# Recommendation tower on one core: products with one selection a chunk, interaction blocks in quarters of 32 rows

## What is computed

```python
e = stack([tbl_f[ids[:, f]] for f in range(39)], axis=1)    # 512 x 39 x 16
# layer 1: all pairs of features, per number d
z = einsum('bmd,bnd->bdmn', e, e).reshape(B, D, 39 * 39)
x1 = einsum('bdp,po->bod', z, W0)                           # 128 outputs
# layer 2: features times the outputs of layer 1
z = einsum('bmd,bnd->bdmn', e, x1).reshape(B, D, 39 * 128)
x2 = einsum('bdp,po->bod', z, W1)
h = concatenate([sum of x1 and x2 over d, dense_ctx], axis=1)   # 272 wide
h = maximum(h @ W_top1 + b_top1, 0)
h = maximum(h @ W_top2 + b_top2, 0)
y = h @ W_top3
```

## Time and profile before

| what | us |
|---|---|
| median of 3 runs | 230.82 (229.24 to 232.3) |
| the profiled execution | 230.19 |
| its span, first to last instruction | 228.6 |
| PE, DVE, ACT, POOL busy | 204.9, 176.5, 167.6, 109.2 |
| first product (L786) | starts at 37.26 |
| last gather (L387) | starts at 141.82 |
| granted clock of TensorE, mean | 0.985 |

### The profile page before, as it was taken

The page is one execution under the profiler, slowest core; times in us unless marked ns, Lnnn a source line. Parts: engine busy times, 40 slices in busy tenths (PEclk is TensorE's granted clock), DMA queues, the critical chain, the costliest instruction groups (busy, mean ns, idle before and its releaser), DMA issues.

```text
span 228.6 us, 4760 instructions
## 1 busy us (share of the span) xinstructions
PE 204.9 (90%) x1715; PEld 156.0 (68%) x1715; DVE 176.5 (77%) x295; ACT 167.6 (73%) x300; POOL 109.2 (48%) x106
## 2 busy tenths in 40 slices
PE   4577956879989998999999899799999999999995
PEld 4577813435556566777787577577778888889794
DVE  0899956999869899999979998798899787532010
ACT  6999465769867999798879998697867575775003
POOL 4788777777777777877777778000000000000000
PEclk9999779999999999999999999999999999999999
DMA  5950000240392591200240000003100000000000
GB/s 143 217 128 7 9 7 6 65 69 6 77 236 66 70 314 29 44 5 7 65 65 7 7 7 7 1 3 94 22 3 0 0 3 0 1 0 3 0 0 3
DMA packets 22015, 10.26 MB, mean 45 GB/s; under 512 B 11576, under 2 KB 20877, under 8 KB 21992
## 3 DMA queue, kind: packets, MB, share of 16 engines
q1 hardware_dynamic: 18728, 9.11, 16.4%
q0 software_dynamic: 3264, 0.84, 3.9%
HBM read 8.63 MB, written 1.31 MB: 44 GB/s over the span
## 4 chain that ended last, share of the span: by engine, by line
PE 60%; DVE 17%; ACT 9%; issue 7%; DMA 4%; POOL 1%; SPq 1%; DVEq 0%; ACTq 0%
PE s_bank L1013 14%; PE side_bank L967 6%; PE side_bank L969 6%; PE side_bank L968 6%; PE g_bank L995 4%; DVE z L786 3%; DVE z_lo L796 3%; DVE w_sb L725 3%; PE b_bank L947 3%; PE side_bank L962 3%; PE side_bank L995 3%; PE side_bank L934 3%; PE side_bank L975 2%; DMA feat<-tbl,ids_sb 2%; PE side_bank L912 2%
## 5 line engine op out<-in xcount | busy, mean ns | idle before, releaser
L387 POOL DMA_INDIRECT feat<-tbl,ids_sb x102 | 109.0, 1069 | 33.3 <-issue 21.9
L575 ACT ACTIVATE z_hi<-z 128x512 fp32r<-128x512 f32 x100 | 61.9, 632 | 10.6 <-DVE z L786 8.7
L786 DVE TENSOR_TENSOR z<-factors,b_bank 128x512 f32<-128x512 f32 x84 | 57.1, 681 | 7.9 <-PE b_bank L947 3.7
L796 DVE TENSOR_TENSOR z_lo<-z,z_hi 128x512 fp32r<-128x512 f32 x84 | 57.8, 688 | 0.3 <-ACT z_hi L575 0.2
L1013 PE MATMUL s_bank<-g,w_sb 128*128 128x128 f32 x312 | 47.5, 279 | 0.0
L1013 PEld LDWEIGHTS s_bank<-g,w_sb 128*128 128x128 f32 x312 | 44.1, 192 | 4.8 <-issue 2.4
L967 PE MATMUL side_bank<-z_hi,w_hi 128*128 128x512 f32 x84 | 42.3, 504 | 0.0
L969 PE MATMUL side_bank<-z_hi,w_lo 128*128 128x512 f32 x84 | 33.2, 396 | 0.0
L968 PE MATMUL side_bank<-z_lo,w_hi 128*128 128x512 f32 x84 | 32.9, 392 | 0.0
L467 ACT ACTIVATE factors<-side_bank 128x512 f32<-128x512 f32 x31 | 18.4, 594 | 7.2 <-PE side_bank L934 7.2
L947 PE MATMUL b_bank<-xs,sel 117*128 117x512 bf16 x48 | 18.7, 389 | 1.4 <-DVE direct_z L786 0.8
(11 more groups left out here) (181 smaller groups left out, 333.0 us busy)
## 6 DMA issues: line engine op xcount, KB each, us to landing
w_sb<-w SPq DMA_DIRECT2D x3, 832.0 KB, 5.8
feat<-tbl,ids_sb POOLq DMA_INDIRECT x102, 2.4
lines<-line SPq DMA_DIRECT2D x4, 320.0 KB, 2.2
diag<-lines SPq DMA_DIRECT2D x32, 40.0 KB
wt_sb<-wt SPq DMA_DIRECT2D x2, 512.0 KB
g<-small SPq DMA_DIRECT2D x1, 770.0 KB
g<-small SPq DMA_DIRECT2D x1, 448.0 KB
w0p<-w_pair SPq DMA_DIRECT2D x1, 448.0 KB
```

The costliest lines, as they stand in the source:

```text
L387: nc.gpsimd.indirect_dma_start(feat[:, bt % 2, n * D:(n + 1) * D], None, tables[order[n]], bass.IndirectOffsetOnAxis(ids_sb[:, bt, n:n + 1 ...
L575: nc.scalar.activation(z_hi[:, s % RING, :], z[:, at, :], ACT.Copy).then_inc(rounded, 1)
L786: nc.vector.tensor_tensor(target, one, other, ALU.mult).then_inc(product, 1)
L796: nc.vector.tensor_sub(low[rows, s % RING, :], z[rows, SPLITS[s] % Z_RING, :], z_hi[rows, s % RING, :].bitcast(f32)).then_inc(remainder, 1)
```

## The change

A partition's list has now four features at most, and all six pairs of the four are used. Three arrays a, b and c are filled and copied to SBUF; the fourth feature is the only selection, in one PSUM bank. The products of a chunk are (a,b), (a,c), (b,c), (a,s), (b,s), (c,s) and the square (a,a), where s is the selection. The ring of factors holds two chunks (three before) of three arrays. Fills and turns use two banks: b and the first half of a turn one of them, a, c and the second half the other, which was the second selection bank. Blocks of g use quarters of 32 rows with 80 columns, 16 matmuls of two passes a chunk in one set with one signal; the side banks come first, and who waits for them waits for the first copy. `diag` has half the size.

```diff
-SELECTS = 3
-BASES = ((0, 5, 10, 13, 20), (0, 14, 3, 16, 21), (0, 8, 12, 14, 17))
-CHAIN = (1, 3, 0, 2, 4)
-LEAD = 2
+COPIES = "abc"
+ARRAYS = len(COPIES) + 1
+ORDER = ((0, 1), (0, 2), (1, 2), (0, 3), (1, 3), (2, 3), (0, 0))
+SELECT_AT = 1
...
-F_RING = 3
+F_RING = 2
...
-BANDS = 2
+BANDS = 4
...
-FILL_A = 4
-FILL_B = 3
+FILL_AT = (2, 3, 5)
...
-A_AT = [0, 24, 25, 25]
-B_AT = [0, 25, 26, 26]
+NEXT_FILL_AT = [(), (25, 26, 26), (25, 26, 26), (25, 26, 26)]
...
-        turn_banks = [turn_bank, g_banks[1], l1_bank[1], b_bank[1][:]]
+        turn_banks = [turn_bank, b_bank[1][:], g_banks[1], l1_bank[0], l1_bank[1]]
...
+        bank_of = {"a": 1, "b": 0, "c": 1}
...
             take_x(0, 0, signal=chunk0_taken)
             take_factor("a", 0)
+            take_factor("c", 0)
             take_x(0, 0, first=CB)
...
-                for half, pair in enumerate((g_bank[:, :, :], side_bank[:, i % 2:i % 2 + 2, :])):
-                    act.wait_ge(g_summed, SETS * i + half + 1)
+                for half, pair in enumerate((side_bank[:, i % 2:i % 2 + 2, :], g_bank[:, :, :])):
+                    act.wait_ge(g_summed, SETS * i + min(half + 1, SETS))
...
-                k, j = u % 2, u // 2
-                if u < 2:
-                    dve.wait_ge(*after(turn_taken, "ab"[u], i, 0))
-                one = factors[:, i % F_RING, k, :]
-                if u == REST_T:
-                    other = one
-                else:
-                    dve.wait_ge(selected, SELECTS * i + j + 1)
-                    other = b_bank[(SELECTS * i + j) % B_RING][:]
+                for k, name in enumerate(COPIES):
+                    if u == max(k - 1, 0):
+                        dve.wait_ge(*after(turn_taken, name, i, 0))
+                if u == len(COPIES):
+                    dve.wait_ge(selected, i + 1)
+                one, other = (factors[:, i % F_RING, k, :] if k < len(COPIES) else b_bank[0][:] for k in ORDER[u])
                 nc.vector.tensor_tensor(target, one, other, ALU.mult).then_inc(product, 1)
...
-                    pe.wait_ge(g_copied, GPC * g_before_fill[n])
+                    pe.wait_ge(g_copied, GPC * g_before_fill[n] - 1)
...
-            def select(i, j):
-
-                q = SELECTS * i + j
-                if j == 0:
-                    features_there(i)
-                if q >= B_RING:
-                    before, number = divmod(q - B_RING, SELECTS)
-                    pe.wait_ge(product, PT * before + 2 * number + 2)
...
+            def select(i):
+
+                features_there(i)
+                if i:
+                    pe.wait_ge(product, PT * (i - 1) + REST_T)
+                nc.tensor.matmul(b_bank[0][:], sel[:, ARRAYS - 1, :], columns(*divmod(i, CPT)),
                                  start=True, stop=True).then_inc(selected, 1)
...
                 if u == 0 and i >= 2:
-                    pe.wait_ge(g_copied, GPC * (i - 1))
+                    pe.wait_ge(g_copied, GPC * (i - 1) - 1)
...
-                        to = [*g_banks, *side][BANDS * (r // SET_SUBS) + h]
+                        to = [*side, *g_banks][BANDS * (r // SET_SUBS) + h]
```

More of the change, by code:

```diff
@@ L49 @@
 LAG = 5
-B_RING = 2
 DIRECT = [[1, 3, 5], [], [], []]
@@ L344, in build @@
                 fills_before_g.append(len(fills[0]))
[L345 to L352, removed]
+            for name, i in factors_due(s):
+                fills[bank_of[name]].append((name, i, 0))
             g_before_fill += [len(fills_before_g)] * (len(fills[0]) - len(g_before_fill))
@@ L658, in _ @@
                     take_xit(i)
[L659 to L662, removed]
+                for name, i in factors_due(s):
+                    if i % CPT:
+                        take_factor(name, i)
                 if 1 <= bt < TILES - 1:
@@ L1182, in _factors, with point @@
 def _factors():
-    rows = [None] * P
-    base_at = [list(range(F)), [*range(F, REST_LO.start), *range(REST_LO.stop, P)], list(range(REST_LO.start, REST_LO.stop))]
-    second = np.zeros(P, bool)
-    for k, base in enumerate(BASES):
-        for n, p in zip(range(F), base_at[k]):
-            rows[p] = [(n + x) % F for x in base]
-            second[p] = k == 1
-    for n, p in zip(range(0, F, 4), base_at[1][F:]):
-        rows[p] = [(n + x) % F for x in CHAIN]
-    factors = np.full((SELECTS + 2, P), -1)
+    def point(i, level):
+        return TURNS * level + i % TURNS
@@ new lines, in _factors @@
+    fixed = [TURNS * LEVELS + k for k in range(F - TURNS * LEVELS)]
+    blocks = [tuple(point(i + n, level) for i, level in block) for block in FOURS for n in range(TURNS)]
+    for k, block in enumerate(THREES):
+        blocks += [(fixed[k], *(point(i + n, level) for i, level in block)) for n in range(TURNS)]
+        blocks += [(fixed[k], *(point(n + step, k) for step in range(0, TURNS, TURNS // 3))) for n in range(TURNS // 3)]
+    blocks.append(tuple(fixed))
+    base_at = [list(range(F)), [*range(F, REST_LO.start), *range(REST_LO.stop, P)][:F], list(range(REST_LO.start, REST_LO.stop))]
@@ new lines, in _factors, with lead @@
+    others = [p for p in range(P) if not any(p in at for at in base_at)]
+    holder = {}
+    def lead(n, tried):
+        for x in blocks[n]:
+            for k in range(len(base_at)):
+                if (x, k) not in tried:
+                    tried.add((x, k))
+                    if (x, k) not in holder or lead(holder[x, k], tried):
+                        holder[x, k] = n
+                        return True
+        return False
+    for n in range(len(blocks)):
+        lead(n, set())
@@ L1199, in _factors @@
+    assert len(holder) == len(base_at) * F
+    rows = {base_at[k][x]: (x, *(y for y in blocks[n] if y != x)) for (x, k), n in holder.items()}
+    rows.update(zip(others, [block for n, block in enumerate(blocks) if n not in holder.values()]))
+    assert len(rows) == len(blocks) <= P
+    second = np.zeros(P, bool)
+    second[base_at[1]] = True
+    factors = np.full((ARRAYS, P), -1)
     pairs = np.full((PT, P, 2), -1)
     seen = set()
-    for p in range(P):
-        if rows[p] is None:
-            continue
-        factors[SELECTS:, p], factors[0:SELECTS, p] = rows[p][0:2], rows[p][2:]
+    for p, row in rows.items():
+        factors[0:len(row), p] = row
@@ L1205, in _factors @@
         for t in range(REST_T):
-            item = tuple(sorted((rows[p][t % 2], rows[p][2 + t // 2])))
-            if item not in seen:
-                seen.add(item)
-                pairs[t, p] = item
+            if max(ORDER[t]) < len(row):
+                item = tuple(sorted(row[k] for k in ORDER[t]))
+                if item not in seen:
+                    seen.add(item)
+                    pairs[t, p] = item
     for at in base_at:
```

74 lines of the change are left out of this document (40 added, 34 removed), and 3 rows, old and new, of the table FOURS.

## The result

The changed kernel takes **236.97 us** (median of 4 runs, 235.98 to 238.19) against 230.22 (229.24 to 232.3) for the kernel before in the same session: a ratio of **1.028, interval 1.023 to 1.033**. It is slower, as forecast, and by less than half of what was forecast: +6.0 us between the two profiled executions (236.22 and 230.19) where the prediction had +13.9. The ratios in this document leave out executions of a slower state wherever enough others are left, so they can differ by some tenths of a per cent from the quotient of the medians.

The account below looks back on a forecast made before the run. The prediction took POOL's gather pace to bound the kernel until 142 us and PE from 151 us. 230.2 + 16 (held gathers) - 0.9 (selections, fills) - 1.2 (blocks) = 244.1, so 244 us, range 229 to 260.

Parts of the forecast that it names:

- What bounds the kernel: Until 142 us POOL's gather issue sets when the last tile can go on; from 151 us PE is full.
- How a gather is held: A gather can't begin inside or between back-to-back DVE operations with two SBUF inputs; operations with a PSUM input don't disturb it.
- How many gathers get out: Up to 142 us, 65 of 78 gathers get out; the 13 missing, at 1.24 us each, cost +16 us.
- 3 + 2 + 1 = 6 a chunk: Gathers per chunk: three in the PSUM steps, two in DVE's gaps, one slipping in at a boundary of two operations.
- Selections and blocks behind the last copy: From 151 us on PE: four fewer selections and fills, -0.9 us; six interaction blocks in quarters, -1.2 us.
- Two banks for fills and turns, the side banks first: Shorter waits for ACT's copies and earlier release of the side banks, ahead of 142 us or beside a full PE: 0.
- ACT's 16 more copies, the other waits: One more factor copy a chunk, 9.5 us, fits in ACT's idle time; waits for selections and ring hidden too: 0.
- The unstarved case: Rival: the gathers are not starved, so only PE's 2 us remain, 228 us; chance 0.22.
- only PE's 2 us: What the change gains if gathers are not delayed: PE's shorter selections, fills and blocks, giving 228 us.
- that rival: Quarters don't run four at a time: blocks grow by up to 0.7 us, +4 over six, 233.3 us; chance 0.04.

Follow-up runs that it names:

- b_few: The kernel before with the gathers of every second feature left out in tiles 1 to 3: 228.37 us, 0.988 of the kernel before.
- a_spread_2: The changed kernel with its steps reordered so that products from SBUF and from PSUM alternate: 230.35 us, 0.998 of the kernel before.
- b_sbuf012_2: The kernel before with products 0, 1 and 2 of each chunk reading SBUF, in one row with the square: 237.72 us, 1.035 of the kernel before.
- b_sbuf135_2: The kernel before with products 1, 3 and 5 of each chunk reading SBUF, spread between the others: 233.45 us, 1.015 of the kernel before.
- a_few: The changed kernel with the gathers of every second feature left out in tiles 1 to 3: 223.29 us, 0.963 of the kernel before.

## Why the prediction was right or wrong

**What bounds the kernel: right.** POOL's pace sets the start of the last tile. After the change the 9.0 us that the gathers take longer are the 9.0 us by which the last copy is late; and b_few, with 39 gathers in the stretch instead of 78, is 1.2% faster than before (0.982 to 0.994).

**How a gather is held: right, and the term that carries the loss.** The rule read from the earlier trace rows held in the changed kernel, at 105.99 as elsewhere. After against a_spread_2 showed that a long row costs what spread ones don't (8.3 us of holding); b_sbuf012_2 against b_sbuf135_2 agrees in sign, with 1.7 us. The Trainium skill ("SBUF — State Buffer", "Who interferes with whom") says that a DVE instruction with two SBUF inputs contends with GpSimd's reads; the traces agree, with up to 4.01 us for a gather of 0.94. The same section's remark that such operations don't stall a DMA issued by GpSimd doesn't hold for these gathers.

**How many gathers get out: this is the step that failed.** "3 + 2 + 1 = 6 a chunk: 65 of 78" and "+16 us". Measured +9.0. The step from missing gathers to time held: 71 of the 78 start by 142 us, and 7 missing x 1.24 = 8.7 us. The count was wrong. The holding can be put in one number. A gather alone is 0.94 us; the 78 after took 90.8, so they were held for 90.8 - 73.3 = 17.5 us in total (8.5 before). The forecast's 16 would have needed 24.5. About ten of the 78 went out in stalls, where nothing holds them; the other 68 were held 0.26 us each. That is one every 0.94 + 0.30 + 0.26 = 1.50 us while DVE runs, 6.4 a chunk of 9.6 us; the forecast's 6 stand for 1.60. The 0.4 a chunk is four or five gathers over the stretch, 5 to 6 of the 7 us of error.

Where they got through can be seen in the trace. The forecast let one a chunk slip in at a boundary of two operations, 11 over the stretch, from a single pair of rows. In the kernel after, 15 gathers start within 0.02 us of the start of a remainder and take 0.94 or 0.95 us (a sixteenth, at 43.59, took 2.71), and 13 of the 15 come in three trains of four, five and four. Part of the train of five, DVE and then POOL:

```profile
122.63 0.72 DVE L801 TENSOR_TENSOR z_lo<-z,z_hi 128x512 fp32r<-128x512 f32 x1
123.28 0.68 DVE L791 TENSOR_TENSOR z<-factors,b_bank 128x512 f32<-128x512 f32 x1
123.88 0.73 DVE L801 TENSOR_TENSOR z_lo<-z,z_hi 128x512 fp32r<-128x512 f32 x1
124.53 0.68 DVE L791 TENSOR_TENSOR z<-factors 128x512 f32<-128x512 f32 x1
125.13 0.72 DVE L801 TENSOR_TENSOR z_lo<-z,z_hi 128x512 fp32r<-128x512 f32 x1
```

```profile
122.63 0.94 POOL L396 DMA_INDIRECT feat<-tbl,ids_sb  x1 [0.30 <-issue]
123.88 0.94 POOL L396 DMA_INDIRECT feat<-tbl,ids_sb  x1 [0.30 <-PE side_bank L969]
125.13 0.94 POOL L396 DMA_INDIRECT feat<-tbl,ids_sb  x1 [0.30 <-issue]
```

A remainder that starts together with a gather is followed by the next operation after 0.65 us instead of 0.60, so two operations take 1.25 us, which is also the distance of two gathers. The next gather then meets a boundary again, and the train runs on even where the products read SBUF only (124.53). The pair of rows that the prediction took for a single slip was part of such a train, from 76.42 to 80.17. That the trains make up the difference to the forecast's 6 is a reading of one trace, not isolated by a run.

**Selections and blocks behind the last copy: right.** Forecast -0.9 - 1.2 = -2.1; measured -2.0 over five chunks, 0.92 from selections and 1.1 from blocks. The quarters run four at a time: passes of the two bank pairs start 0.01 us apart, rounds 0.11, a block 1.07 us against 1.08 forecast. Each block saves 0.22; five count, not six, since the gain of the sixth (0.23) is lost again just in front of it. On this the Trainium skill ("TensorE: Matmul & The Clock Gate") has two rules that pull apart, concurrency of row tiles in Part 3 and the cost of a load in Part 2. Here four tiles run together, which agrees with Part 3, and their loads don't queue one behind the other. Rounds come at 0.11 us although 80 columns would take 0.07 by the earlier trace rows; that the loads set this pace, as the prediction had it, fits Part 2 and was not tested.

**Two banks for fills and turns, the side banks first: valued at 0, worth 0.9.** The cover named for it ("ahead of 142 us, or beside a full PE") didn't hold at one place: the turn of the last tile lies just behind the last gather, when PE is not full but waits for ACT's copy of g. Its first half starts 0.58 us sooner behind the last copy and its second half another 0.31. A wait shortened ahead of the limiting event is worth nothing, the same wait right behind it all of its length.

**ACT's 16 more copies, the other waits: 0, right.** ACT has 85.8 of 104.6 us in the stretch; in a_few, where nothing else holds it up, 94.8 of 104.6 and all of the 9 us to 151, and the kernel still gains. It may be the next limit.

**The rivals.** The unstarved case was given 0.22 and 228 us. It is what a_spread_2 nearly shows, 228.8 us in the profiled execution and 230.35 in the median, but only with the other order. For the change without the pull of the gathers its sign was right, and its size too small: a_few gained 5.1 us on b_few by the medians and 4.2 by the spans, where "only PE's 2 us" were expected. The quarters do run four at a time, so that rival is out.

## What to carry to other kernels

Before moving operands from PSUM to SBUF, look at what GpSimd does at the time. If its pace sets a later stage, two-input SBUF operations should not stand in rows; put the ones that read PSUM between them: the order alone took this change from 2.8% slower to no slower. And a saving counts from the point where the limiting event has passed: cut the trace there, and price each half by itself.

## What the runs showed of the hardware

- A waiting gather isn't let in between back-to-back operations with two SBUF inputs: one waited through five boundaries, 3.07 us (105.99 to 109.06). One that starts just as an operation begins mostly gets in (15 of 16 at the start of a remainder after); the remainder then takes 0.72 to 0.74 instead of 0.68 us, and the gathers behind it can follow in step.
- A stall that leaves PE idle can be followed by a stretch in which part of the time is at the lower clock level: mean clock 0.81 and 0.72 in the 12 us after stalls of 2.76 and 2.24 us. In the changed kernel the block at 72.03, behind the stall of 7.60 us, has its first passes at 0.50 us instead of 0.34; the mean clock from 66 to 72 us is 0.50. Not each stall does it: after the 3.53 us at 149.28 in b_sbuf012_2 the clock stays up.
- Four row groups of 32 with 80 columns each run at once at 0.11 us a round; a block of 32 such passes takes 1.07 us against 1.29 for 16 passes in halves.
- The kernel before takes 229.9 to 231.3 us in three of the sessions and 253.8 in the fourth, on another chip; the trace of the changed kernel from there has pauses of over 3 us that no engine of the core accounts for.
